# Row statistics, decay table and routing constants moved to other steps of a fused AdaLN attention, MoE and FFN kernel

## The reference, cut to what matters

```
# 1: multi-query attention, 16 heads of 64, one shared k and v, one null key and value
xn  = ln(x, g_norm)
q   = l2norm(xn @ Wq) * q_scale;   k = l2norm(concat(null_k, xn @ Wk)) * k_scale
sim = q @ k.T * 8 + rel_pos_bias(n)           # bias: a small MLP over relative positions
a   = ln(softmax(masked sim) @ v @ Wout, g_out)
# 2: linear attention with decay
decay   = sigmoid(decay_logit)
expo    = maximum(pos[None, :] - pos[:, None] - 1, 0)
weights = decay ** expo * (pos[None, :] > pos[:, None])
x = x + ((a @ Wq.T) @ (a @ Wk.T).T / 16 * weights) @ (a @ Wv.T) @ Wo.T * out_scale
# 3 and 4: 8 experts, top 2 of them, with shared experts; then a ReLU FFN 256 -> 1024 -> 256
x = x + ffn(moe(x, cond))
```

## Time and profile before

| | before |
|---|---|
| median of 3 runs | 520.21 us (519.82 to 521.36) |
| profiled execution | 520.21 us |
| its span, first to last instruction | 518.7 us |
| TensorE busy | 462.6 us (89%) |
| VectorE | 337.4 us (65%) |
| GpSimd | 278.5 us (54%) |
| ScalarE | 259.6 us (50%) |
| mean granted TensorE clock | 0.947 |
| HBM traffic | 100 GB/s over the span |

### The profile page before, as it was taken

How to read it: one execution, slowest core, us unless ns; L and a number is a source line. 1 busy time by engine, 2 the same in 40 slices (tenths; PEclk the granted TensorE clock), 3 DMA queues, 4 the chain that set the end, 5 groups by cost and what they waited for, 6 DMA issues and landing times.

```text
span 518.7 us, 11676 instructions
## 1 busy us (share of the span) xinstructions
PE 462.6 (89%) x4029; PEld 409.0 (79%) x4029; DVE 337.4 (65%) x827; ACT 259.6 (50%) x514; POOL 278.5 (54%) x300
## 2 busy tenths in 40 slices
PE   6785988999999999999989684799999399999997
PEld 4674887888898988888878573698997279898986
DVE  5887898888888888887462471667674425453522
ACT  4665465656676666665421021366654145343442
POOL 5779888988979798977247266000000542516000
PEclk9999899999999999999986778699999889999999
DMA  7741019082736400101013122545652211303011
GB/s 249 154 155 33 1 27 348 5 289 86 253 121 215 159 30 0 30 1 33 1 41 111 42 79 85 191 125 174 226 163 101 83 43 39 96 27 104 24 37 40
DMA packets 51662, 52.16 MB, mean 101 GB/s; under 512 B 6692, under 2 KB 49062, under 8 KB 51624
## 3 DMA queue, kind: packets, MB, share of 16 engines
q1 hardware_dynamic: 48004, 42.98, 25.9%
q0 software_dynamic: 3072, 8.39, 5.0%
q10 hardware_dynamic: 548, 0.28, 0.2%
HBM read 22.03 MB, written 29.62 MB: 100 GB/s over the span
## 4 chain that ended last, share of the span: by engine, by line
PE 41%; POOL 18%; DVE 16%; issue 13%; another core or an unknown queue 5%; ACT 5%; DMA 1%; DVEq 0%; POOLq 0%; ACTq 0%
PE bank L330 6%; PE bank L331 6%; PE bank L332 6%; PE bank L335 5%; PE bank L336 4%; POOL sim L598 4%; POOL rn L603 4%; POOL pr L583 4%; PE bank L1706 3%; DVE den L1067 2%; DVE qn L1061 2%; ACT oT_h L749 2%; POOL wu_l L570 2%; DVE oT_l L1053 1%
## 5 line engine op out<-in xcount | busy, mean ns | idle before, releaser
L621 POOL DMA_INDIRECT yg<-slot_y,yrow x32 | 34.3, 1071 | 123.6 <-DMA slot_y<-yb 78.7
L603 POOL TENSOR_TENSOR rn<-sc,half 128x6 f32<-128x6 f32 (+1 forms) x48 | 60.1, 1275 | 2.8 <-DVE sc L1042 1.8
L1283 DVE TENSOR_TENSOR hl<-hw,hh 128x512 fp32r<-128x512 f32 x32 | 22.2, 692 | 57.7 <-ACT hw L874 52.5
L872 ACT ACTIVATE hh<-bank,late 128x512 fp32r<-128x512 f32 x32 | 22.0, 689 | 54.1 <-PE bank L1706 41.8
L612 POOL DMA_INDIRECT slot_x<-xs,posi x32 | 31.7, 990 | 21.3 <-DVE posi L1145 12.2
L335 PE MATMUL bank<-wout_h,oT_h 128*128 128x256 f32 x128 | 34.1, 302 | 6.7 <-DVE oT_l L1053 6.7
L583 POOL TENSOR_TENSOR pr<-pe,rden 128x1024 f32<-128x1024 f32 x16 | 30.5, 1904 | 13.4 <-DVE rden L1070 12.5
L330 PE MATMUL bank<-wqkv_h,xnT_h 128*128 128x384 f32 x96 | 35.3, 368 | 1.8 <-DVE sim L1028 1.1
L598 POOL TENSOR_TENSOR sim<-sim,mx 128x1040 f32<-128x1040 f32 x16 | 30.9, 1933 | 10.0 <-DVE mx L1031 9.9
L566 POOL TENSOR_TENSOR biasm<-bias,mneg 128x1040 f32<-128x1040 f32 x16 | 35.7, 2233 | 0.1
L336 PE MATMUL bank<-wout_l,oT_h 128*128 128x256 f32 x128 | 32.8, 292 | 0.0
(11 more groups left out here) (311 smaller groups left out, 1560.6 us busy)
## 6 DMA issues: line engine op xcount, KB each, us to landing
slot_x<-zrow SPq DMA_DIRECT2D x4, 4352.0 KB, 14.5
xq<-slot_x SPq DMA_DIRECT2D x40, 128.0 KB, 2.0
slot_y<-yb SPq DMA_DIRECT2D x20, 256.0 KB, 2.3
fstage<-in_f_W SPq DMA_DIRECT2D x4, 512.0 KB, 4.2
out<-p_all SPq DMA_DIRECT2D x8, 256.0 KB, 2.1
raw_out<-in_c_Wout SPq DMA_DIRECT2D x2, 512.0 KB, 7.9
xs<-in_x SPq DMA_DIRECT2D x1, 1024.0 KB, 7.7
stage<-in_m_wgate SPq DMA_DIRECT2D x8, 128.0 KB
```

Of the source, the lines that this page charges most:

```text
L603: e.tensor_tensor(rn[:, lo:hi], sc[:, lo:hi], half[:, lo:hi], ALU.pow).then_inc(sems['rn'], 1)
L621: e.indirect_dma_start(out=yg[:, g % 2, r, t, :], out_offset=None, in_=ydram.ap()[:, :], in_offset=bass.IndirectOffsetOnAxis(ap=yrow[:, g ...
```

## The change

It does this:

- The first split of the x load is smaller: tiles 2 and 3 before the bias ladder, tiles 4 to 15 after the attention weights. Group 2 of the row statistics (tiles 4 to 7) now waits for the late load.
- `row_stats(2)` moves in step 0 from ahead of the score additions to behind `fold_keys`; `row_stats(3)` and `(4)` move from the ends of steps 1 and 2 to ahead of the row sums of the same steps.
- The decay table is made in six places instead of one: the exponential after step 0 (`decay_exp`, ScalarE), the sum ahead of the row sums of step 1 (`decay_sum`, VectorE), the logarithm after step 1 (`decay_log`), clamps, sum and sign ahead of the row sums of step 2 (`decay_rate`, VectorE, with the clamp of the table that GpSimd did before), the power after step 2 (`decay_power`), and the mask on GpSimd after step 2.
- `slot_constants` is joined to `route_constants`, after step 14.

Without the unchanged lines:

```diff
--- before.py
+++ after.py
@@ -359,7 +359,7 @@
-            e.dma_start(xs[:, 2:8, :], x_v[:, 2:8, :]).then_inc(sems['ld_x1'], 16)
+            e.dma_start(xs[:, 2:4, :], x_v[:, 2:4, :]).then_inc(sems['ld_x1'], 16)
@@ -372,7 +372,7 @@
-            e.dma_start(xs[:, 8:NT, :], x_v[:, 8:NT, :]).then_inc(sems['ld_x2'], 16)
+            e.dma_start(xs[:, 4:NT, :], x_v[:, 4:NT, :]).then_inc(sems['ld_x2'], 16)
@@ -480,8 +480,6 @@
-                e.tensor_scalar(decay[:, :], decay[:, :], 0.0, None, ALU.max).then_inc(sems['pc'], 1)
-                e.wait_ge(sems['pc'], upto('pc'))
@@ -492,9 +490,8 @@
-                e.iota(iota_j[:, :], pattern=[[1, SLOTS]], base=0, channel_multiplier=0, allow_small_or_imprecise_dtypes=True).then_inc(sems['p_const'], 1)
-
-            def slot_constants():
+                e.iota(iota_j[:, :], pattern=[[1, SLOTS]], base=0, channel_multiplier=0, allow_small_or_imprecise_dtypes=True).then_inc(sems['pc'], 1)
+                e.wait_ge(sems['pc'], upto('pc'))
@@ -540,7 +537,6 @@
-                mask_decay()
@@ -552,7 +548,7 @@
             def mask_decay():
-                e.wait_ge(sems['a_decay'], 4)
+                e.wait_ge(sems['a_decay'], 3)
@@ -603,7 +599,7 @@
-            pipeline(e, body, {-2: after_norm0, -1: after_first_projection, 0: after_first_scores, 1: after_second_scores, NT - 2: route_constants, NT - 1: slot_constants})
+            pipeline(e, body, {-2: after_norm0, -1: after_first_projection, 0: after_first_scores, 1: after_second_scores, 2: mask_decay, NT - 2: route_constants})
@@ -672,20 +668,22 @@
-
-            def decay_power():
-                e.wait_ge(sems['v_decay'], 2)
-                e.wait_ge(sems['p_const'], 1)
+            before_squares = {-1: before_first_squares, 1: wvo_upper, NT: lambda: x_upper(1)}
+
+            def decay_exp():
+                e.wait_ge(sems['v_decay'], 1)
...
-                e.activation(col(LNA), col(EXA), ACT.Ln, bias=ones[:, 0:1].bitcast(F32)).then_inc(sems['a_decay'], 1)
+
+            def decay_log():
+                e.wait_ge(sems['v_decay'], 2)
+                e.activation(col(LNA), col(EX1), ACT.Ln).then_inc(sems['a_decay'], 1)
...
-                e.activation(col(LND), col(LNA), ACT.Identity, bias=col(MXN), scale=-1.0).then_inc(sems['a_decay'], 1)
-                e.wait_ge(sems['a_decay'], upto('a_decay'))
+
+            def decay_power():
+                e.wait_ge(sems['v_decay'], 3)
...
-
-            before_squares = {-1: before_first_squares, 0: decay_power, 1: wvo_upper, NT: lambda: x_upper(1)}
@@ -780,7 +778,7 @@
-            pipeline(e, body, {-1: lambda: wout_upper(1), 2: wt_upper, NT - 1: first_x, NT: lambda: router_exp(0), NT + 1: lambda: x_upper(2)})
+            pipeline(e, body, {-1: lambda: wout_upper(1), 0: decay_exp, 1: decay_log, 2: lambda: [decay_power(), wt_upper()], NT - 1: first_x, NT: lambda: router_exp(0), NT + 1: lambda: x_upper(2)})
@@ -909,9 +907,7 @@
-                e.tensor_scalar(col(MXN), col(NX), 0.0, -1.0, ALU.max, ALU.mult).then_inc(sems['v_decay'], 1)
...
-                e.wait_ge(sems['v_decay'], upto('v_decay'))
@@ -957,15 +953,32 @@
+            def decay_rate():
+                e.wait_ge(sems['p_const'], 1)
+                e.tensor_scalar(decay[:, :], decay[:, :], 0.0, None, ALU.max).then_inc(sems['vc'], 1)
+                e.wait_ge(sems['vc'], upto('vc'))
+                e.tensor_scalar(col(MXN), col(NX), 0.0, None, ALU.max).then_inc(sems['vc'], 1)
+                e.wait_ge(sems['vc'], upto('vc'))
+                e.wait_ge(sems['a_decay'], 2)
+                e.tensor_tensor(col(LND), col(LNA), col(MXN), ALU.add).then_inc(sems['vc'], 1)
+                e.wait_ge(sems['vc'], upto('vc'))
+                e.tensor_scalar(col(LND), col(LND), -1.0, None, ALU.mult).then_inc(sems['v_decay'], 1)
+                e.wait_ge(sems['v_decay'], upto('v_decay'))
+
...
+            def decay_sum():
+                e.wait_ge(sems['a_decay'], 1)
+                e.tensor_scalar(col(EX1), col(EXA), 1.0, None, ALU.add).then_inc(sems['v_decay'], 1)
+                e.wait_ge(sems['v_decay'], upto('v_decay'))
+
...
-            before_retrieval = {0: lambda: row_stats(2), 3: decay_ready}
+            before_retrieval = {3: decay_ready}
@@ -983,14 +996,14 @@
-            before_sums = {-1: before_first_sums, 3: lambda: [wvo_lower(), wt_lower()], NT: lambda: x_lower(1), NT + 1: lambda: router_places(0)}
+            before_sums = {-1: before_first_sums, 1: lambda: [decay_sum(), row_stats(3)], 2: lambda: [decay_rate(), row_stats(4)], 3: lambda: [wvo_lower(), wt_lower()], NT: lambda: x_lower(1), NT + 1: lambda: router_places(0)}
...
-            before_norms = {0: fold_keys}
-            after_v = {-1: lambda: [wout_lower(), row_stats(1)], 0: fold_vo, 1: lambda: row_stats(3), 2: lambda: row_stats(4)}
+            before_norms = {0: lambda: [fold_keys(), row_stats(2)]}
+            after_v = {-1: lambda: [wout_lower(), row_stats(1)], 0: fold_vo}
...
             def row_stats(n):
...
-                e.wait_ge(sems[('ld_x0', 'ld_x1', 'ld_x1', 'ld_x2', 'ld_x2')[n]], 16 * 1)
+                e.wait_ge(sems[('ld_x0', 'ld_x1', 'ld_x2', 'ld_x2', 'ld_x2')[n]], 16 * 1)
@@ -1130,7 +1143,7 @@
-                e.wait_ge(sems['p_const'], 3)
+                e.wait_ge(sems['p_const'], 2)
```

## The result

The changed kernel takes 527.4 us (median of 4 runs, 525.36 to 528.24) against 520.08 us (4 runs): ratio 1.0121, interval 1.0082 to 1.0162. It is slower. In all 24 executions of the changed kernel from that time the median is 526.6 us. Timed again later it had 524.68 (12 runs) against 520.9 us, ratio 1.0076 [1.0045, 1.0107]. The forecast, 525.0 over 520.2, is 1.0092 and lies between the two. A few executions of a kernel are in a slower state (5 of 29 of the kernel before, 525.0 to 525.9 us), and every ratio leaves them out.

The account below looks back on a forecast made before the run. Time lost in the first steps' chain of small operations delays the part where TensorE is saturated. The sum was 520.2 + 3.1 (steps 0 to 3) + 1.7 (step 15) = 525.0 us, range 520.3 to 527.6.

Parts of the forecast that it names:

- Step 0: First pipeline step: score additions 0.5 us earlier, row_stats(2) later in the way; together +0.3 us.
- Step 1: Second pipeline step: row_stats(3) and decay_sum nearly covered by a wait for ScalarE; zero, bounds 0 and +0.4 us.
- Step 2: VectorE before the row sums: decay_rate held until GpSimd's L598 ends, row_stats(4) behind it; rn +3.1 us.
- the table load before pe: ScalarE in step 2: a load before its Exp, 0.5 us on the path.
- The wait at nm: GpSimd in step 3 waiting for mv, the projection's statistics: the 1.01 us wait goes.
- Its lower bound: Step 2 if no operation is held by L598: 2.0 us less; for steps 0 to 3 together, 0.7.
- (a): Rival, step 2: L598 holds nothing of decay_rate; L598 of step 3 0.7 us late, 522.6 us; chance 0.13.
- Step 15: Routing constants' memsets, 1.84 us, ahead of pr on GpSimd: saturated TensorE, slack 0.15, stands still 1.7 us.
- rival b: Projections of steps 3 and 4: TensorE's clock falls again, first fall hidden, second not; +1.6, 526.6 us; chance 0.2.
- (c): Rival: not slower, statistics free in new places, sc of step 2 ending with L598; 520.4 or 519.3 us; chance 0.17.

Follow-up runs that it names:

- stats first: Changed kernel with row_stats(4) ahead of decay_rate on VectorE in step 2; ratio 1.0085 to the kernel before.
- one input: Changed kernel with decay_rate's last two operations (sum of two columns, sign) made one tensor_scalar; median 525.31 us, ratio 1.0076.
- stats alone: Kernel before the change with only the x load split and the row statistics moved; ratio 0.9990.
- second profile: Changed kernel, unaltered, run and profiled once more beside the kernel before; ratio 1.0076.
- more clamps: Changed kernel with decay_rate's one-column clamp done seven times instead of once, ahead of the sum; ratio 1.0089.

## Why the prediction was right

Point by point, with the shifts of the profiled execution:

- **Step 0.** Forecast: start 0.5 us earlier, pr 0.3 later. L1028 (now L1041) started at 28.25 and pr at 41.71; with the first matmul 0.75 late by chance (3.11 us; in nine of the eleven experiments 2.34 to 2.49) that is 0.25 earlier and 0.55 later. biasm then waited for the bias DMA, which the prediction had as the next in line.
- **Step 1: nothing.** L598 of step 1 to that of step 2: 14.72 us against 14.67. Other executions with the changed steps 0 and 1 had 14.02 to 15.27.
- **Step 2.** The forecast of 3.1 us for rn is on the clock of the profile and has the 0.3 of step 0 in it; against L598 it is 2.8, and 2.77 came. pr +3.7: 11.97 - 8.64 = +3.33; the table load before pe put 0.29 us on the path, not 0.5. The wait at nm was to go wholly, 1.01 us; 0.48 remained (see the clock). rsx, the scale of later x tiles that GpSimd takes between nm and L598 of step 3 (L513, now L510), took 1.01 us instead of 1.42, which was not in the forecast. So the total of steps 0 to 2 (2.98 for 3.1) is partly luck: step 0 cost 0.53 up to L598 of step 1 and not 0.3, and step 2 2.40 and not 2.8. L598 of step 3 was forecast 3.1 late and came 3.73 late, 2.98 without the start. The prediction held that one operation of decay_rate would be stretched to the end of L598 and left open which; it was the one with two inputs. Its lower bound does not follow: 3.1 less 2.0 is 1.1, not the 0.7 that (a) has. Without the hold (stats first) step 2 was 17.73 us long, 1.1 more than before the change.
- **Step 15.** 1.7 us: 1.86, and 1.76 to 1.82 in six further executions with that order. pr of step 15 came 1.99 us later against L598 of step 14, a little more than the 1.84 of the memsets, and all but 0.13 of it reached pr of step 16: the slack of 0.15 us is about right.
- **The clock** (rival b). It fell once more at step 3's projection (5.60 us instead of 4.06) and not at step 4's: after a wait of 1.07 us the clock stayed at 1.00. (b) held the first fall to be hidden. It was not quite: VectorE waited 1.44 us for this block before the statistics, and the 0.48 us at nm are what came through; where the statistics stood in the same place and the clock stayed at 1.00 (one input, stats alone), nm had no wait. The 0.2 us in step 3 (13.55 against 13.32) are not the clock's. In every execution with 13.53 to 13.55 the sc of 128x5 came into L598 and was held (1.49 to 1.56 us), so that the first rn waited for it; in all those with 13.32 or 13.33 it passed in 0.17 us, and only the next sc was held.
- **What was missing.** The profiled executions differ by 7.9 us, the forecast has 4.8. The other 3.1 are 0.75 of start, 0.2 of step 3, 0.15 of step 15 and 2.1 behind pr of step 16, less 0.1 in steps 0 to 2; the median lies 0.7 below that execution. The late first matmul and the longer rest didn't come again in the second profile, which had 1.2 us more up to L598(0) instead, and rest alone varied from 269.3 to 274.2 us on one chip among kernels that are alike in it. That is spread, for which the range was there, and no term of the sum.

The rivals: (a), nothing held, falls with the 1.67 us; (c), not slower, was right about the statistics (-0.7 us in step 2 by themselves) and wrong for this kernel since decay_rate stands before them. Up to L598 of step 3 the statistics alone gained 0.27 us, not 1.5, as steps 0 and 1 took most of it back.

## What to carry over

Before you put a small operation into a gap of one engine, look at what the other engines do in that gap: 128 additions cost 1.67 us beside GpSimd's subtraction, 0.16 beside nothing, and what was free behind them no longer was. Work that is cheap at a point where its engine waits (memsets before a 1.86 us wait) is paid in full at a point where the engine feeds a saturated one. When a kernel's runs spread by 5 us, cut its profiles at common instructions: in steps 2 and 3 and up to step 16 the price of a part was the same to 0.1 us in nearly every kernel (more clamps differ by 0.24 in step 2), while the medians could hardly tell it. The stretches before and behind are not so steady: there one profile shows nothing.

## What had not been expected of the hardware

- Beside the same GpSimd operation, L598, a 128x1 tensor_scalar took 0.15 us, while the 128x5 tensor_scalar of L1042 took up to 1.64 us (its 1.83 us was beside wout_l), a 128x1 tensor_tensor 1.67 and a 128x16 one 1.94. Form and shape decide, not size alone. All 16 slow L1042 of the kernel before end 0.02 to 0.03 us behind a tensor_tensor of GpSimd. Why the five columns wait and one doesn't was not tried.
- TensorE's clock in the output projection blocks of steps 2 to 4, by the idle time before them, in all 13 profiles: after 0.65 to 1.77 us (23 blocks) it was 1.00. After 1.81 and 2.00 us it was 0.85 and 0.83 over the first 2 us and 0.50 over the next 2. After 2.25 to 3.42 us it was 0.50 to 0.77 over the first 2 us. Over 5.6 us the 16 blocks behind 1.81 us and more had 0.70 to 0.75.
- The two chips differ by 12.3 us for the same kernel (520.08 and 507.75), and the difference lies in "rest". In the first profile of before, the router's first VectorE operation of the second batch waited 8.5 us for something that the profile calls remote (5.0 to 9.2 in every profile of this chip); on the other it waited 1.5 to 3.4 us for TensorE. What it is stays open.

```profile
292.16 0.29 DVE L1108 TENSOR_REDUCE lg<-bank 128x64 f32<-128x128 f32 x1 [8.49 <-remote]
```
